# Expert tiles with one bias sum on VectorE, HH written in place, a reordered start and reciprocals before the last rows

## The reference, cut to what matters

```python
xn = _layernorm(x)
h = _rmsnorm(xn, norm_scale)
q, k, v = (einsum('bsd,dhe->bshe', h, w) for w in (wq, wk, wv))
weights = softmax(einsum('bqhd,bkhd->bhqk', q * 64 ** -0.5, k))
attn = einsum('bqhe,hed->bqd', einsum('bhqk,bkhd->bqhd', weights, v), w_out) + b_out
logits = silu(xn @ rw1 + rb1) @ rw2 + rb2
k_prob, k_index = softmax(top_k(logits, 2))
for e in range(8):                       # hidden width 512
    we = sum(where(k_index == e, k_prob, 0))
    out += we * (silu(xn @ w1[e] + b1[e]) @ w2[e] + b2[e])
x + attn + out
```

## Time and profile before

| what | value |
|---|---|
| three runs | 1893.66, 1896.05, 1896.06 us (median 1896.05) |
| the profiled execution | 1897.43 us |
| its span, first to last instruction | 1895.6 us (1.8 us less than its time) |
| PE busy, and PE weight loads | 1837.4 us (97%), 1150.4 us (61%) |
| DVE busy | 1627.9 us (86%) |
| ACT busy | 1200.1 us (63%) |
| POOL busy | 713.6 us (38%) |
| granted TensorE clock, mean | 0.995 |

### The profile page before, as it was taken

The page is one execution under the profiler, slowest core; times in us unless marked ns, Lnnn a source line. Parts: engine busy times, 40 slices in busy tenths (PEclk is TensorE's granted clock), DMA queues, the critical chain, the costliest instruction groups (busy, mean ns, idle before and its releaser), DMA issues.

```text
span 1895.6 us, 74352 instructions
## 1 busy us (share of the span) xinstructions
PE 1837.4 (97%) x32434; PEld 1150.4 (61%) x32434; DVE 1627.9 (86%) x2297; ACT 1200.1 (63%) x2969; POOL 713.6 (38%) x623
## 2 busy tenths in 40 slices
PE   8999999999999999998999999999999999999997
PEld 4555555555555555554566666666676666666665
DVE  6999999999999999989888888888888888888885
ACT  5666776666666666664666675756666766666662
POOL 2344554435444445432023324324334333333242
PEclk9999999999999999999999999999999999999998
DMA  2133321111111111111434334343333434333342
GB/s 85 32 82 109 96 93 57 43 39 45 37 47 48 48 48 47 27 42 54 110 74 83 83 72 89 78 84 77 90 72 66 102 73 86 74 79 65 81 77 50
DMA packets 154485, 130.13 MB, mean 69 GB/s; under 512 B 27664, under 2 KB 139024, under 8 KB 154128
## 3 DMA queue, kind: packets, MB, share of 16 engines
q1 hardware_dynamic: 123568, 104.65, 20.0%
q0 software_dynamic: 30592, 20.73, 8.3%
HBM read 93.15 MB, written 34.27 MB: 67 GB/s over the span
## 4 chain that ended last, share of the span: by engine, by line
PE 47%; ACT 24%; DVE 17%; issue 11%; DMA 1%; SPq 0%; POOL 0%; ACTq 0%; DVEq 0%; POOLq 0%
ACT PR L896 16%; PE pair L329 10%; PE pair L310 9%; PE pair L469 8%; DVE NM L550 7%; DVE PT L558 4%; PE pair L342 4%; PE pair L295 4%; ACT ZT L979 3%; ACT ZZ L982 3%; PE pair L385 3%; PE pair L283 2%; DVE OT L567 2%; PE pair L271 2%; PE pair L239 1%
## 5 line engine op out<-in xcount | busy, mean ns | idle before, releaser
L896 ACT ACTIVATE PR<-pair,NM 128x512 f32<-128x512 f32 x1024 | 696.3, 697 | 542.2 <-DVE NM L550 541.8
L558 DVE STREAM_TRANSPOSE PT<-PR 128x1024 f32<-128x1024 f32 x512 | 633.2, 1241 | 119.0 <-ACT PR L896 105.5
L550 DVE TENSOR_REDUCE NM<-pair 128x2 f32<-128x1024 f32 x512 | 598.1, 1208 | 23.1 <-PE pair L310 23.1
L310 PE MATMUL pair<-KS,QS 64*32 64x512 f32 x8192 | 503.1, 598 | 12.3 <-ACT PR L896 9.4
L329 PE MATMUL pair<-PT,V 32*64 32x256 f32 x16384 | 478.7, 378 | 12.6 <-ACT ZZ L982 9.7
L1139 POOL DMA_INDIRECT out<-YS,IDW x156 | 249.9, 1602 | 607.2 <-DVE YS L813 382.0
L329 PEld LDWEIGHTS pair<-PT,V 32*64 32x64 f32 x16384 | 375.9, 131 | 166.3 <-issue 103.0
L310 PEld LDWEIGHTS pair<-KS,QS 64*32 64x32 f32 x8192 | 124.0, 106 | 253.6 <-issue 151.7
L896 ACT ACTIVATION_READ_ACCUMULATOR PR<-pair,NM 128x1 f32 x1024 | 218.9, 214 | 0.0
L979 ACT ACTIVATE ZT<-pair,BT 128x512 f32<-128x512 f32 x156 | 109.8, 704 | 111.5 <-PE pair L224 111.4
L1086 POOL TENSOR_TENSOR TH<-TH,HS 128x512 f32<-128x512 f32 x64 | 82.1, 1283 | 230.7 <-ACT HS L935 230.7
(11 more groups left out here) (121 smaller groups left out, 1693.2 us busy)
## 6 DMA issues: line engine op xcount, KB each, us to landing
RB<-l_rows SPq DMA_DIRECT2D x128, 256.0 KB, 4.3
E<-w_tab SPq DMA_DIRECT2D x39, 512.0 KB, 4.7
XG<-slots SPq DMA_DIRECT2D x39, 264.0 KB, 4.2
E<-in_w SPq DMA_DIRECT2D x39, 256.0 KB, 3.7
xin<-in_x SPq DMA_DIRECT2D x16, 256.0 KB, 2.9
XQ<-in_x SPq DMA_DIRECT2D x16, 256.0 KB, 3.2
l_rows<-RT SPq DMA_DIRECT2D x256, 2.0 KB
w_tab<-SPL SPq DMA_DIRECT2D x8, 512.0 KB, 2.6
```

Of the source, the lines that this page charges most:

```text
L310: m = pe.do.matmul(bank[2 * (s % 2) + r][32 * c:32 * c + 32, :], QS[rows, u % 2, c, at:at + 32], KS[rows, g % 2, c, :], start=True, stop=T ...
L550: dve.do.tensor_reduce(NM[:, step % 4], pairs[s % 2][:], AX.X, ALU.max, negate=True).then_inc(sem["dve_max"])
L558: dve.do.transpose(PT[:].rearrange("p c k q -> p (c k) q")[:, :, 32 * slot:32 * slot + 32], PR[:, step % PRB].rearrange("p r k -> p (r k)" ...
L896: act.do.activation(PR[:, step % PRB, r, :], bank[2 * (s % 2) + r], ACT.Exp, bias=NM[:, step % 4, r:r + 1], accum_out=RS[:, g % 2, r, at:a ...
```

## The change

1. Quarters 0 to 2: ACT writes z + bias straight into HH, and `halves` reads and writes HH; the buffer ZZ is gone.
2. Quarter 3: DVE makes z + bias from PSUM (`last_quarter`, new L804), after its `halves` of quarters 0 and 1. ACT's tanh of quarter 3 waits for it, and PE's bank is given back by that tanh.
3. At the start, POOL's `routed_rows(0)` waits for the four `first_rows` of DVE; WARM is 12, not 16; `turn_x(0)` comes after the first scores on PE and at G = 1 on ACT.
4. The last unit's `denominators` move from G = 256 to G = 255, ahead of the last `give_back`.

```diff
--- before.py
+++ after.py
...
@@ -31,7 +31,7 @@
 PRB = 3
 BIG = 1.0e30
 ROW = 132
-WARM = 16
+WARM = 12
 WSPLIT = 24
 LOADS = "id wk0 wk1 wq0 wq1 wv0 wv1 ns r10 rb1 r2 rb2 consts tri wo bo tiles bias".split()
 SEMS = (["load_" + name for name in LOADS] + """
@@ -158,7 +158,6 @@
-        ZZ = sb("ZZ", [P, 4, S])
@@ -457,7 +456,10 @@
                 pe.wait_ge(*side("e1", i))
                 came_free(bk)
                 three(pe, bank[bk], w, m).then_inc(sem["pe_h1"])
-                free[bk] = sem["act_zz"], NC * i + c + 1
+                if c == NC - 1:
+                    free[bk] = sem["act_zt"], NC * i + c + 1
+                else:
+                    free[bk] = sem["act_zz"], (NC - 1) * i + c + 1
 
             def expert_out(i):
                 bk = ring.take(("w2", i))
@@ -490,12 +492,13 @@
                 keys(0, c)
                 if c % 2:
                     queries(0, c // 2)
-            turn_x(0)
             for G in range(TIMES + 8):
                 u, k = divmod(G, 4)
                 if u < UNITS:
                     scores(u, 2 * k)
                     scores(u, 2 * k + 1)
+                if G == 0:
+                    turn_x(0)
                 if k < 2 and 0 < u <= UNITS:
                     weighted(u - 1, k)
                 routing(G)
@@ -794,12 +797,21 @@
                 dve.wait_ge(sem["pe_h1"], NC * (i - 1))
                 dve.do.tensor_tensor(X2[:, i % 2, 1], bank[BANK["xg", i]], X2[:, i % 2, 0], ALU.subtract).then_inc(sem["dve_xl"])
 
+            def last_quarter(i):
+                dve.wait_ge(sem["pe_h1"], NC * i + NC)
+                dve.wait_ge(sem[f"bt_{i % 3}"], 32 * (i // 3 + 1))
+                dve.wait_ge(sem["pe_w2"], i - 1)
+                dve.do.tensor_scalar(HH[:, i % 2, NC - 1], bank[BANK["h1", i, NC - 1]], BT[:, i % 3, NC - 1:NC], None,
+                                     ALU.add).then_inc(sem["dve_z"])
+
             def halves(i, c):
                 n = i * NC + c
                 dve.wait_ge(sem["act_zt"], n + 1)
-                dve.wait_ge(sem["act_zz"], n + 1)
-                dve.wait_ge(sem["pe_w2"], i - 1)
-                dve.do.scalar_tensor_tensor(HH[:, i % 2, c], ZT[:, n % 2], 1.0, ZZ[:, n % 4], ALU.add, ALU.mult).then_inc(sem["dve_s"])
+                if c == NC - 1:
+                    dve.wait_ge(sem["dve_z"], i + 1)
+                else:
+                    dve.wait_ge(sem["act_zz"], (NC - 1) * i + c + 1)
+                dve.do.scalar_tensor_tensor(HH[:, i % 2, c], ZT[:, n % 2], 1.0, HH[:, i % 2, c], ALU.add, ALU.mult).then_inc(sem["dve_s"])
 
             def give_back(i):
                 dve.wait_ge(sem["pe_w2"], i + 1)
@@ -823,6 +835,8 @@
                         give_back(i)
                     if what == "h" and c[0] < 2:
                         halves(i, c[0])
+                    if what == "h" and c[0] == NC - 1:
+                        last_quarter(i)
 
             dve.do.memset(junk[:], 0.5).then_inc(sem["dve_junk"])
             dve.do.memset(ONES[:], 1.0).then_inc(sem["dve_one"])
@@ -837,7 +851,7 @@
             dve.do.memset(PM[:, 0, 0], 0.0).then_inc(sem["dve_pm0"])
             for G in range(TIMES + 8):
                 u, k = divmod(G, 4)
-                if k == 0 and 0 < u <= UNITS:
+                if k == 0 and 0 < u < UNITS:
                     denominators(u - 1)
                 if k == 2 and 0 < u <= UNITS:
                     weighted(u - 1)
@@ -856,6 +870,8 @@
                 route(G)
                 if k == 2 and 0 < u <= UNITS:
                     project_out(u - 1)
+                if G == TIMES - 1:
+                    denominators(u)
                 experts(G)
 
         @block.scalar
@@ -976,10 +992,13 @@
                 act.wait_ge(*biases(i))
                 if n >= 2:
                     act.wait_ge(sem["dve_s"], n - 1)
+                if c == NC - 1:
+                    act.wait_ge(sem["dve_z"], i + 1)
                 act.do.activation(ZT[:, n % 2], ps, ACT.Tanh, bias=BT[:, i % 3, 8 + c:9 + c], scale=0.5).then_inc(sem["act_zt"])
-                if n >= 4:
-                    act.wait_ge(sem["dve_s"], n - 3)
-                act.do.activation(ZZ[:, n % 4], ps, ACT.Identity, bias=BT[:, i % 3, c:c + 1]).then_inc(sem["act_zz"])
+                if c == NC - 1:
+                    return
+                act.wait_ge(sem["pe_w2"], i - 1)
+                act.do.activation(HH[:, i % 2, c], ps, ACT.Identity, bias=BT[:, i % 3, c:c + 1]).then_inc(sem["act_zz"])
 
             def experts(G):
                 for i, what, *c in PLAN[G]:
@@ -994,9 +1013,10 @@
                 keys(0, c)
                 if c % 2:
                     queries(0, c // 2)
-            turn_x(0)
             for G in range(TIMES + 8):
                 u, k = divmod(G, 4)
+                if G == 1:
+                    turn_x(0)
                 if u < UNITS:
                     probs(u, 2 * k)
                     if k == 2 and u + 1 < UNITS:
@@ -1154,6 +1174,7 @@
             pool.do.memset(HALF[:], -0.5).then_inc(sem["pool_half"])
             power(0)
             pool.do.memset(XR[:].rearrange("p a k t d -> p (a k t) d")[:, :, D:ROW], 0.0).then_inc(sem["pool_spare"])
+            pool.wait_ge(sem["dve_hc"], QT)
             routed_rows(0)
             pool.do.memset(PAD[:], 0.0).then_inc(sem["pool_pad0"])
             pool.wait_ge(sem["pool_pad0"], 1)
@@ -1279,7 +1300,9 @@
                 if i >= 2:
                     sp.wait_ge(sem["pe_h1"], NC * (i - 1))
                 if i >= 3:
-                    sp.wait_ge(sem["act_zz"], NC * (i - 2))
+                    sp.wait_ge(sem["act_zz"], (NC - 1) * (i - 2))
+                    sp.wait_ge(sem["act_zt"], NC * (i - 2))
+                    sp.wait_ge(sem["dve_z"], i - 2)
                     sp.wait_ge(sem["dve_y"], i - 2)
                 ex = sp.do.value_load(REG[:, i:i + 1], min_val=0, max_val=E - 1)
                 sp.do.dma_start(E1[:, i % 2].rearrange("p a c -> p (a c)").bitcast(F32),
```

More of the change, by code:

```diff
@@ L43 @@
     dve_OT dve_ri dve_rt dve_acc dve_sum dve_gate dve_pm dve_at dve_pk dve_row dve_to dve_wt dve_tot
-    dve_xl dve_s dve_y dve_ys dve_rb1h dve_pm0 dve_hf
+    dve_xl dve_s dve_z dve_y dve_ys dve_rb1h dve_pm0 dve_hf
     act_xTs act_V act_k act_q act_exp act_th act_hz act_tanh act_shi act_xh act_lgs act_zt act_zz
```

## The result

The changed kernel takes **1903.24 us** (median of 6 runs, 1901.14 to 1904.4), beside it the kernel before 1895.92 us (6 runs, 1893.39 to 1897.62). The ratio is 1.0040, its 95% interval 1.0029 to 1.0052: 7.3 us slower, more than the 0.2% that can be told from no change. The forecast was 1901.7 us, inside 1893.5 to 1908.5. The profiled execution took 1904.4 us.

A forecast was written before the change was run, and what follows sets the result against it. The DVE/ACT chain was taken to set the time after slots, with PE paying where it lacks slack. Slots +10.6, start -2.6 and end -2.4 gave +5.6 us: 1901.7 us forecast, range 1893.5 to 1908.5.

The forecast's parts named there:

- The sum, +5.6: Whole kernel: slots +10.6, start -2.6, end with last slot -2.4, together +5.6 us.
- HH in place: zero: Quarters written into HH instead of ZZ: no wait becomes later, so zero, bounds -0.05 and +0.05 us per slot.
- +0.43 in a slot: Slots at G = 226 or 230 and their like: exponentials start at 1675.00 in place of 1674.57, held by DVE.
- The rule that speaks against the part: Skill rule to optimize the fullest engine first; by it alone, loading DVE (86%) would cost the upper bound of 25 us.
- 10 units at G % 8 = 3: Unit ends there: 0.52 slack against 0.58 delay, the rest paid at OT, less where `finish` stands between; 3.1 us in all.
- The start, -2.6: Kernel start: quicker `first_rows` and shorter warm-up let PE turn HR at 9.62 in place of 12.18; bounds 0 and -3.1.
- The end, -2.4 with the last slot: Kernel end: earlier reciprocals bring OT 2.5 earlier, `finish` runs into the read-back at 1889.7; bounds 0 and -3.
- more isn't to be had, because of that read: Kernel end: SP's read-back of the sums caps the gain, even if PE's last product ran faster.
- PE's queue hides it: Rival for the slots: PE's queue hides the new DVE instruction, slots +4.4, 1895.5 us; chance 0.24.
- everything pays: Rival for the slots: all 29 unit ends pay 0.65, 18.9 in all, 1910 us; chance 0.12.
- The start or the end gives nothing: Rival for start and end: one gain missing gives 1904.5 us, both missing 1907; chance 0.10.
- ACT was the limit: Rival for the slots: last ZZ's bank comes 0.5 earlier ten times if DVE is kept under 0.25, 1886 us; chance 0.07.

The follow-up runs named there:

- e1: Kernel before with only HH in place and quarter 3's sum on DVE, start and end as before: 1908.22 us, ratio 1.0058 to 1.0085.
- e4: Changed kernel with ACT making all four sums into HH, no new DVE instruction: 1892.1 us, ratio to before 0.9972 to 0.9990.
- e9: e1 with DVE's quarter 3 sum one place earlier, between the first and second `halves`: 1891.43 us, ratio to before 0.9968 to 0.9986.
- e2: Kernel before with only the new start (POOL held back, WARM 12, `turn_x(0)` later): 1893.62 us, ratio 0.9989 to 1.0007.
- e7: Kernel before with only the new start, but WARM left at 16: 1895.71 us, ratio 0.9982 to 1.0007.
- e8: Kernel before with only the new start, but `turn_x(0)` left ahead of the first scores: 1895.05 us, ratio 0.9988 to 1.0011.
- e5: Changed kernel with DVE's quarter 3 sum one place earlier, between the first and second `halves`: 1886.59 us, ratio to before 0.9939 to 0.9970.
- e10: e6 with a third ZT buffer for tanh results: 1883.21 us, ratio to before 0.9932 to 0.9959.
- e3: Kernel before with only the last unit's reciprocals moved ahead of the last `give_back`: 1891.74 us, ratio 0.9976 to 0.9994.
- e11: e4 with a third ZT buffer for tanh results: 1892.12 us, ratio to before 0.9972 to 0.9990.
- e6: Changed kernel with DVE making the first quarter's sum instead of the last, ahead of the first `halves`: 1894.58 us, ratio to before 0.9980 to 1.0004.
- e12: e10's kernel run again, beside e11 on the same chip: 1883.07 us, ratio to before 0.9918 to 0.9948.

## Why the prediction was right, point by point

**The sum, +5.6.** It came out near because misses of opposite sign met. In the two traces the slots cost 13.1 (2.5 more than forecast, 1.0 of it the clock at G = 139), the start kept 1.9 (0.7 less), and the end gave 4.3 (1.9 more). That these nearly cancel is luck. What isn't luck is the main term: the bias part alone (e1) has +11.5 in its trace and +12.7 by the medians for the forecast 10.6, in the kinds of slot and by the waits that were named.

**HH in place: zero.** Right (e4: 0.00 in every kind of slot).

**The price of the instruction and +0.43 in a slot.** Right: L804 keeps DVE for 0.67, and what arrives at the exponentials is 0.47 (5.05 against 4.58), since ACT had been 0.15 late before. Units at G % 8 = 7: 0.43, as worked out from the earlier trace rows. Double slots: 0.42 and -0.06, as from the earlier trace rows.

The rule that speaks against the part gave too much. By the Trainium skill, Perfetto Trace Analysis, section "Identifying the Most-Contended Engine", DVE at 86% is the engine to relieve first. The price of 39 more instructions that hide nowhere was 25; e1 shows 12.7, and e9, with the same load on DVE, a gain. Here the place in the queue counted, and not the busy share.

**10 units at G % 8 = 3: the term that was mis-sized.** I had 3.1 and the trace has 5.0 (e1's has 4.1); undisturbed ones pay 0.46 to 0.48 each, whether `finish` stands between or not. Two steps of it failed. From the view in order of time of the changed kernel, the slot at G = 226, its unit's end at G = 227, and OT at G = 230:

```profile
1656.99 1.12 ACT L919 COPY V<-pair 128x512 f32<-128x512 f32 x2
1658.21 3.71 PE L328 MATMUL pair<-PT,V 32*64 32x256 f32 x128 [0.27 <-DVE PT L561]
...
1667.37 1.95 PE L309 MATMUL pair<-KS,QS 64*32 64x512 f32 x32
1668.68 1.25 DVE L570 TENSOR_TENSOR OT<-pair,RB 128x512 f32<-128x512 f32 x2
1669.39 0.66 PE L238 MATMUL pair<-idn,acc 128*128 128x128 f32 x4
```

- I read 0.52 of slack between the transposition and PE in the earlier trace rows. But PE also needs the bank that ACT's copy of V frees. That copy stands behind the exponentials, ends at 1658.11, and is as late as they are; PE follows 0.1 behind. The view names the transposition, but that one ended 0.24 before. In all these units of this trace PE starts 0.10 or 0.21 behind the copy, and 0.33 to 0.42 later in the slot than before, where I had 0.1 (the last unit has no such copy, and two were disturbed).
- I gave the five units with `finish` 0.5 of slack, because its products (L238) stand between on PE. They wait for OT themselves: 1669.39 is 0.71 behind OT's start, when the first half is done. The bank that they write is the one that OT frees. So these pay in full: 5 x 0.27 too little, 1.4 of the 1.9.

**The start, -2.6.** The mechanism is shown. The size differs from one execution to the next, and one loss was not foreseen:

```profile
1.70 7.43 PE L489 MATMUL pair<-PR 128*128 128x256 f32 x24 [1.70 <-DVE PR L844]
7.90 1.11 DVE L537 TENSOR_SCALAR HR<-xin,mv,sqo 128x128 f32<-128x128 f32 x4 [1.88 <-POOL sqo L1044]
9.07 0.66 PE L238 MATMUL pair<-idn,HR 128*128 128x128 f32 x4
9.10 1.04 POOL L1066 TENSOR_TENSOR XR<-XQ,mv 128x512 f32<-128x512 f32 x1 [1.17 <-DVE HR L537]
```

The four `first_rows` take 1.11 together instead of 4.02, with POOL's first multiplication (L1066) held back until they are done; nothing else was changed for them, and it is 1.11 or 1.12 in e2, e7 and e8 too. This is what the Trainium skill says in SBUF — State Buffer, section "Who interferes with whom", of a port pair that VectorE and GpSimd share, and the trace agrees. PE turns HR at 9.07, not 9.62: the warm-up ended 0.5 earlier than I had read off, and the rows were done at 9.01, as forecast, so it is 3.1 at the first scores. In the nine traces with 12 calls the 24 products took 7.28 us (e5) to 8.49 us (e10): they come every 0.43 us at first and every 0.22 later, the switch lies at another moment in each, and the granted clock reads 1.00 on both sides of it. With it the gain at the first scores runs from 2.2 (e10) to 3.1, and 2.6 lies inside. What I hadn't seen is that 1.2 of the 3.1 were gone at G = 139. Most of that has two rows, an OT at G = 10 and one at G = 26 that now wait for their RB, which didn't bind before:

```profile
79.09 1.29 DVE L570 TENSOR_TENSOR OT<-pair,RB 128x512 f32<-128x512 f32 x2 [0.35 <-DMA RB<-l_rows]
184.22 1.29 DVE L570 TENSOR_TENSOR OT<-pair,RB 128x512 f32<-128x512 f32 x2 [0.59 <-DMA RB<-l_rows]
```

The first stands in this trace alone and costs 0.5. The second comes with the change, at least with its 12 calls: in all nine traces with 12 calls, e2 among them, the OT at G = 26 waits for RB (0.59 to 1.02 us) and 0.7 to 1.1 us are lost there, and in the five with 16 calls (before, e1, e3, e7, e9) it never waits. e7, with the rest of the new start, begins 1.7 earlier and loses nothing there. Why the detour through DRAM comes late at that place after the earlier start isn't shown. e2 still had 2.8 at G = 255, since it won back 0.4 elsewhere.

**The end, -2.4 with the last slot.** The detour went as worked out. The changed kernel's end, in order of time:

```profile
1879.88 5.35 PE L471 MATMUL pair<-E,HH 128*128 128x128 f32 x32 [3.46 <-DVE HH L814]
1882.02 0.21 DVE L579 RECIPROCAL RI<-RS 128x16 f32<-128x16 f32 x1
1886.11 4.96 PE L328 MATMUL pair<-PT,V 32*64 32x256 f32 x164 [0.88 <-DVE YS L821]
1891.64 2.84 PE L328 MATMUL pair<-PT,V 32*64 32x256 f32 x92 [0.57 <-issue]
1894.56 1.29 DVE L570 TENSOR_TENSOR OT<-pair,RB 128x512 f32<-128x512 f32 x2 [7.87 <-PE pair L328]
1895.90 1.99 PE L341 MATMUL pair<-OT,WO 128*128 128x256 f32 x8 [1.43 <-DVE OT L570]
1896.00 0.41 SPq L1375 DMA_DIRECT2D xin<-out  x1
1899.11 0.69 DVE L613 TENSOR_TENSOR xin<-pair,xin 128x512 f32<-128x512 f32 x1 [0.75 <-PE pair L238]
```

Against the earlier trace rows, OT waits for PE and no longer for RB, and is 2.8 earlier if counted from the last slot (forecast 2.5). That these two agree so well is partly luck: the last second product took 5.35 for 6.75, and `weighted` took 8.4 for 7.23, with a pause of 0.57 in it for which the profile shows no wait (e5 and e11 have such a pause too), and the two nearly cancel. The rest came from a place that I hadn't priced. PE was idle for 4.57 in front of the last projection before and for 1.43 now, and the projection took 3.47 before, mostly at the 1.2 GHz level (granted 0.50 from 1888 to 1890), and 1.99 now, at the 2.4 GHz level (the last projection of before, then the windows view of the changed kernel over its own):

```profile
1887.45 3.47 PE L342 MATMUL pair<-OT,WO 128*128 128x256 f32 x8 [4.57 <-DVE OT L567]
```

```profile
1896.00:1898.00 2.00, 1.90 (x8) 1.34 (x8) 0.07 (x1) 0.00 (x0) 0.00 (x0) 1.00 0.38 114
```

The step that failed is "more isn't to be had, because of that read": here the read-back landed at 1898.6, before `finish` wanted it at 1899.11. The limit exists all the same. In e3 `finish` does wait for the read:

```profile
1878.17 1.29 DVE L567 TENSOR_TENSOR OT<-pair,RB 128x512 f32<-128x512 f32 x2 [6.68 <-PE pair L329]
1880.88 0.41 SPq L1354 DMA_DIRECT2D xin<-out  x1
1883.73 0.69 DVE L610 TENSOR_TENSOR xin<-pair,xin 128x512 f32<-128x512 f32 x1 [1.77 <-DMA xin<-out]
```

**The rivals.** "PE's queue hides it" and "everything pays" fell with e1 (+12.7, between their 4.4 and 18.9). "The start or the end gives nothing" fell with e3 for the end; for the start only the traces speak, and its medians can't be told from nothing. "ACT was the limit" is the interesting one. I let it win only if the new instruction kept DVE less than 0.25 us. Its mechanism, ten banks 0.5 earlier, was real: e5 and e9 show nine times 0.52. What it needed was not a quicker instruction but a place in DVE's queue where DVE was idle; that condition I drew too narrowly.

## What to carry to other kernels

Before an instruction is moved to another engine, find the idle time of that engine in the same stage and put the instruction into it, one place ahead of the wait and not behind it: one place in the queue was worth some 16 us here (e1 against e9), and turned a loss of 12.7 into a gain of about 4. When an engine then gets ahead, look at what it waits for next (here the second of two buffers), because the gain can stop there unseen. And a copy that stands behind the delayed work on its engine is delayed with it, so slack is counted to the last of all the releasers of a wait, not to the one that the view names. Last, a sum that comes out near doesn't vouch for its terms: compare them one by one.

## What the runs showed of the hardware that I had not expected

The granted clock near the end differs between executions after the same idle time. PE waits 2.86 us for the last `halves` ahead of its last second product in the kernel before and in e3, and the level differs. One row of the view in order of time and one of the windows view, of before first, of e3 below:

```profile
1868.03 6.75 PE L469 MATMUL pair<-E,HH 128*128 128x128 f32 x32 [2.86 <-DVE HH L802]
...
1871.00:1873.00 2.00, 2.00 (x11) 2.00 (x11) 0.00 (x0) 0.00 (x0) 0.00 (x0) 0.50 0.00 0
```

```profile
1866.19 3.06 PE L469 MATMUL pair<-E,HH 128*128 128x128 f32 x25 [2.86 <-DVE HH L802]
...
1866.00:1868.00 2.00, 1.81 (x16) 1.81 (x17) 2.00 (x3) 0.81 (x4) 1.56 (x1) 1.00 0.36 33
```

In the first the clock lay at the 1.2 GHz level (0.50) and the 32 products took 6.75 us; in the second it stayed at 2.4 GHz and all 32 took 3.84. e4 and e11 differ by a buffer that nothing waits for, both with 2.86 of idle time ahead, and took 3.84 and 5.47. Over all traces it was 3.84 in six (e3, e4, e6, e9, e10, e12) and 5.35 to 6.75 in the eight others. So up to 2.9 us of the end of a single trace is this; e3's end, 6.6 shorter in its trace, holds 2.9 of it, and the medians say 3 to 4.

In front of the last projection the level goes with the idle time in every trace: with 3.9 to 4.6 us of it the projection took 3.4 to 3.8, at a mean granted clock of 0.50 to 0.58 (before, e1, e2, e7, e8, e9), with 1.4 it took 1.99, at 1.00 (the changed kernel and all with early reciprocals, eight traces). That is some 1.5 us which the moved reciprocals bring beside their detour, where the read-back doesn't take it back. What decides the level ahead of the second product stays open.
